# One tile in 48 fetched row by row by SyncE, beside GpSimd's gathers

## The reference

```
layer 0 (GCN):  S h, times W1, relu, S again, times W2      S: sum over edges with degree factors
layer 1:        total(h) - sum_{edges} h[src], normalized, times W
layer 2 (GCN):  edge weights edge_weight, one sum over edges
layer 3:        per edge a function of x[src], x[dst], batch norm, softmax-like weights, sum at dst
```

## Time and profile before

| | |
|---|---|
| Median of 3 runs | 11316.48 us (11309.37 to 11317.57) |
| The profiled execution | 11348.41 us, its span 11346.6 us |
| Mean granted TensorE clock | 0.597 |
| Busy: PE, PEld, DVE, ACT, POOL | 38%, 26%, 30%, 28%, 73% |
| Gathers of pass 0, 1, 2, 3, 4 begin at | 267.6, 2373.3, 4386.4, 6458.8, 8569.6 us |
| The last gather of pass 3, of pass 4 starts at | 8420.0, 10557.1 us |
| DMA, mean over the span | 94 GB/s |

### The profile page before, as it was taken

The page is one execution under the profiler, slowest core; times in us unless marked ns, Lnnn a source line. Parts: engine busy times, 40 slices in busy tenths (PEclk is TensorE's granted clock), DMA queues, the critical chain, the costliest instruction groups (busy, mean ns, idle before and its releaser), DMA issues. The chain is left out here.

```text
span 11346.6 us, 83949 instructions
## 1 busy us (share of the span) xinstructions
PE 4273.1 (38%) x19462; PEld 3000.1 (26%) x19463; DVE 3429.0 (30%) x7384; ACT 3213.0 (28%) x7261; POOL 8251.9 (73%) x8365
## 2 busy tenths in 40 slices
PE   1222222342222223223333433333354333334687
PEld 0111111121111112111111333333354333333576
DVE  4000001110001112000000422222235677777898
ACT  3333333343333334333333300000021111111465
POOL 5777777757777775777777677777766777777676
PEclk5555555665555555555555665655676555555799
DMA  4222222232222223222222212221214555555454
GB/s 104 78 79 79 79 79 79 74 87 79 79 79 79 79 79 100 78 79 79 78 78 78 62 52 52 52 52 53 53 46 137 156 159 164 164 164 168 149 168 134
DMA packets 676090, 1067.87 MB, mean 94 GB/s; under 512 B 150850, under 2 KB 518729, under 8 KB 648857
## 3 DMA queue, kind: packets, MB, share of 16 engines
q0 software_dynamic: 329072, 676.05, 22.8%
q10 hardware_dynamic: 247712, 225.10, 6.1%
q1 hardware_dynamic: 98985, 163.50, 4.4%
HBM read 904.63 MB, written 161.05 MB: 94 GB/s over the span
## 5 line engine op out<-in xcount | busy, mean ns | idle before, releaser
L447 POOL DMA_INDIRECT big<-table_parts,tile_cols x4689 | 4453.3, 950 | 1593.1 <-issue 1428.9
L604 PE MATMUL psum<-big 128*128 x4992 | 1724.3, 504 | 4129.3 <-SPq L456 4030.3
L604 PEld LDWEIGHTS psum<-big 128*128 128x128 bf16 x4992 | 663.9, 140 | 4928.4 <-issue 2683.2
L447 POOL DMA_INDIRECT big<-ptable,tile_cols x1563 | 1512.1, 967 | 498.7 <-issue 476.3
L447 POOL DMA_INDIRECT big<-table,tile_cols x1563 | 1485.9, 951 | 478.7 <-issue 476.2
L561 ACT ACTIVATE big<-big,ones 128x2048 bf16<-128x2048 bf16 x312 | 624.4, 2001 | 3707.5 <-PE psum L604 2469.5
L554 ACT ACTIVATE big<-iota_col,dl_tab 128x128 bf16<-128x128 f32 x4992 | 1490.6, 387 | 33.7 <-PEq L731 13.3
L1617 PE MATMUL psum<-acc,big 128*128 x3328 | 788.4, 420 | 1217.5 <-DVE big L1594 1205.1
L583 DVE TENSOR_REDUCE acc<-psum 128x128 f32<-128x384 f32 (+1 forms) x196 | 109.7, 560 | 3648.4 <-PE psum L608 1829.2
L677 PE MATMUL psum<-big 128*128 x3328 | 751.9, 418 | 1201.8 <-SPq L456 750.1
L1617 PEld LDWEIGHTS psum<-acc,big 128*128 128x128 f32 x3328 | 704.9, 317 | 1300.9 <-issue 1300.6
(11 more groups left out here) (300 smaller groups left out, 4274.1 us busy)
## 6 DMA issues: line engine op xcount, KB each, us to landing
big<-dl_rows ACTq DMA_DIRECT2D x104, 1024.0 KB
zrows<-big ACTq DMA_DIRECT2D x104, 1024.0 KB
big<-zrows SPq DMA_DIRECT2D x104, 1024.0 KB
big<-table_parts,tile_cols POOLq DMA_INDIRECT x4689, 2.6
table_parts<-big SPq DMA_DIRECT2D x42, 672.0 KB, 3.5
big<-table,tile_cols POOLq DMA_INDIRECT x1563, 2.5
big<-ptable,tile_cols POOLq DMA_INDIRECT x1563, 2.6
ptable<-big SPq DMA_DIRECT2D x14, 455.0 KB, 3.9
```

Source lines behind the costliest of these rows:

```text
L447: pool.indirect_dma_start(out=slots[:, t % (groups * GT), 0:width], out_offset=None, in_=tab, in_offset=bass.IndirectOffsetOnAxis(ap=idx_t ...
L604: last = nc.tensor.matmul(held, m, rows_t, start=False, stop=False, skip_group_check=True)
```

## The change

In passes 0 to 3, POOL leaves the last tile of 31 groups (8, 14, 20, ..., 188) to SP. For that tile SP issues 128 transfers, each of one row from DRAM into one partition of the ring's slot. They are spread over the six relay steps that lie between the release of the slot (group 8 + 6k uses the slots of group 6k) and the relay's landing of that group: 21 or 22 transfers in each step, behind the step's `s_free`. The byte offsets of the 128 rows are in a new table in SBUF, made once in the setup (row numbers times 768, and times 512 for pass 3), and SP loads them into registers 32 at a time. The transfers share one semaphore, `s_side`, that the relay waits for (16 x 128) and clears ahead of announcing the group. SP's part is written out, as it was; TensorE's programs stay loops. In the setup, SP issues two more loads ahead of the copies, and DVE waits for them and makes two multiplications.

```diff
+SIDE_FIRST, SIDE_EVERY = 8, 6
+SIDE_LOAD = 32
...
+    SIDE = list(range(SIDE_FIRST, TGROUPS - RGROUPS + LEAD + 1, SIDE_EVERY))
+    SIDE_SPAN = SIDE_EVERY * GT * P
+    SIDE_BASE = (SIDE_FIRST + 1) * GT * P - SIDE_SPAN
...
+        def has_side(no, g):
+            return no < PASSES - 1 and g in SIDE
...
-            return 16 * sum(tiles_of(k) for n in range(no + 1)
+            return 16 * sum(tiles_of(k) - has_side(n, k) for n in range(no + 1)
...
-                for k in range(tiles_of(g)):
+                for k in range(tiles_of(g) - has_side(no, g)):
...
-        def relay_rows(sp, no, groups, lead, s_done, done0):
+        def relay_rows(sp, no, groups, lead, s_done, done0, fetch_side=None):
             def landed(g):
                 sp.wait_ge(gathered[g % RGROUPS], landed_count(no, g))
+                if has_side(no, g):
+                    sp.wait_ge(s_side, 16 * P)
+                    sp.sem_clear(s_side)
                 sp.sem_inc(s_landed[no], 1)
...
                     sp.sem_inc(s_free, 1)
+                    if fetch_side:
+                        fetch_side(sp, g)
+
+        def side_rows(no, tab, slots, width, kind, row_bytes):
+            flat, size = tab.rearrange("n f -> (n f)").unsqueeze(0), row_bytes // width
+            numbers = []
+            def fetch(sp, g):
+                k, j = g // SIDE_EVERY, g % SIDE_EVERY
+                if k >= len(SIDE):
+                    return
+                t = SIDE[k] * GT + GT - 1
+                for e in range(j * P // SIDE_EVERY, (j + 1) * P // SIDE_EVERY):
+                    if e % SIDE_LOAD == 0:
+                        numbers.clear()
+                        words = [nc.alloc_registers(f"side{no}_{k}_{e + i}", engines=[SP]) for i in range(SIDE_LOAD)]
+                        nc.regs_load(words, side_of[kind][k:k + 1, e:e + SIDE_LOAD])
+                        numbers.extend(nc.snap(word, engines=[SP], donate=True, min_val=0, max_val=(N - 1) * row_bytes,
+                                               guaranteed_mod_val=0, out_of_modulus=row_bytes) for word in words)
+                    at = numbers[e % SIDE_LOAD] // size
+                    sp.dma_start(slots[e:e + 1, t % RSLOTS, 0:width], flat[:, bass.ds(at, width)]).then_inc(s_side, 16)
+            return fetch
...
-                    relay_rows(sp, no, RGROUPS, LEAD, s_prod, items0)
+                    relay_rows(sp, no, RGROUPS, LEAD, s_prod, items0, side_rows(no, table16, ring16, NPARTS * F, 0, 2 * NPARTS * F))
...
+                side_src = src[SIDE_BASE:SIDE_BASE + len(SIDE) * SIDE_SPAN].rearrange("(k s) -> k s", s=SIDE_SPAN)[:, SIDE_SPAN - P:]
+                for to in side_of:
+                    sp.dma_start(to, side_src).then_inc(s_last, 16)
...
-                dve.wait_ge(s_last, 32)
+                dve.wait_ge(s_last, 64)
+                nc.vector.tensor_scalar(side_of[0], side_of[0], 2 * NPARTS * F, None, ALU.mult)
+                step(nc.vector.tensor_scalar(side_of[1], side_of[1], 4 * F, None, ALU.mult))
```

More of the change, by code:

```diff
@@ L77, in gnn_kernel @@
     NTAB = NI + BODY
+    SIDE = list(range(SIDE_FIRST, TGROUPS - RGROUPS + LEAD + 1, SIDE_EVERY))
+    SIDE_SPAN = SIDE_EVERY * GT * P
+    SIDE_BASE = (SIDE_FIRST + 1) * GT * P - SIDE_SPAN
+    assert SIDE_FIRST == RGROUPS and RGROUPS - SIDE_EVERY == LEAD and SIDE_BASE + len(SIDE) * SIDE_SPAN <= E
     CHUNKS = NW // CW
@@ L180, in gnn_kernel @@
         score_tab = ew_tab[:, 0:NI]
+        side_tab = sb("side_numbers", [64 + len(SIDE), P], i32)
+        side_of = [side_tab[64 * k:64 * k + len(SIDE), :] for k in range(2)]
         rows_all = sb("rows", [13, max(7 * SCW, NI // 2, PLAN_HALVES * PLAN_WORDS)])
@@ L429, in gnn_kernel @@
         s_free = sem("rows_free")
+        s_side = sem("side_rows")
         def tiles_of(g):
             return min(GT, NT - g * GT)
+        def has_side(no, g):
+            return no < PASSES - 1 and g in SIDE
         def landed_count(no, g):
-            return 16 * sum(tiles_of(k) for n in range(no + 1)
+            return 16 * sum(tiles_of(k) - has_side(n, k) for n in range(no + 1)
                             for k in range(g % RGROUPS, g + 1 if n == no else TGROUPS, RGROUPS))
@@ L632, in _ @@
                 def _(sp):
-                    relay_rows(sp, no, RGROUPS, LEAD, s_prod, items0)
+                    relay_rows(sp, no, RGROUPS, LEAD, s_prod, items0, side_rows(no, table, ring32, F, 1, 4 * F))
                 @block.vector
@@ L914, in _ @@
                         ln.relu(act, t - 1, (t - 1) % 2)
-                act.wait_ge(s_dve, 15)
+                act.wait_ge(s_dve, 16)
                 nc.scalar.activation(deg_r, deg, ACT.Sqrt).then_inc(s_cnt, 1)
@@ L934, in _ @@
                 nc.vector.tensor_scalar(is_node[:], node_id[:, 0:NW], float(N), None, ALU.is_lt)
-                dve.wait_ge(s_last, 32)
-                step = Steps(dve, s_dve, 0, 3)
+                dve.wait_ge(s_last, 64)
+                nc.vector.tensor_scalar(side_of[0], side_of[0], 2 * NPARTS * F, None, ALU.mult)
+                step = Steps(dve, s_dve, 0, 4)
+                step(nc.vector.tensor_scalar(side_of[1], side_of[1], 4 * F, None, ALU.mult))
                 nc.vector.tensor_scalar(last_wi, last_i, P.bit_length() - 1, None, ALU.arith_shift_right)
@@ L951, in _ @@
                 dve.wait_ge(s_starts, 1)
-                step = Steps(dve, s_dve, 3, 10)
+                step = Steps(dve, s_dve, 4, 10)
                 step(nc.vector.tensor_tensor(bound[:, 0:NW], bank[5][:, 0:NW], wplus1[:, 0:NW], ALU.add))
@@ L1035, in _ @@
                         keep_dl(t - 2)
-                step = Steps(dve, s_dve, 3 + 10, 3)
+                step = Steps(dve, s_dve, 4 + 10, 3)
                 dve.wait_ge(s_degrees, 1)
@@ L1063, in _ @@
                 last.then_inc(s_counted, 1)
-                pe.wait_ge(s_dve, 3)
+                pe.wait_ge(s_dve, 4)
                 nc.tensor.matmul(bank[5][:, 0:NW], first, tile_cnt[:, 1:NW + 1], start=True, stop=True).then_inc(s_starts, 1)
```

## The result

The changed kernel takes 11159.99 us (median of 4 runs, 11154.31 to 11165.72) against 11317.02 (4 runs, 11309.37 to 11317.73) for the kernel before on the same chip: a ratio of 0.9864, 95% interval 0.9848 to 0.9879. The forecast was 11164.0. The profiled execution spans 11159.8 us.

The account below looks back on a forecast made before the run. POOL's gathers were taken as the bound. Profiled: 11348.4 - 155.6 for 124 tiles + 3 for setup = 11195.8 us; the same 152.6 off the median 11316.5 gives 11163.9, whole range 11140 to 11800.

Parts of the forecast that it names:

- What goes: POOL's gathers in passes 0 to 3: 124 tiles fewer at 1.2549 us each, 155.6 us off.
- The pace: SP's time for six groups against POOL's for 47 tiles: 59.65 us against 59.0, so SP 0.65 behind.
- T: SP's time for six groups, with 128 row transfers, register loads, relay and waits: forecast 59.65 us.
- the law: A pass loses side tiles x (T - POOL's cycle) - slack where positive; forecast as 31 x (T - 59.0) - 49 us.
- The slack: SP frees ring slots five groups ahead of POOL's need: some 49 us, covering a lag of 20 us at a pass's end.
- The address without an operation: SP's row transfers: division and multiplication of the number cancel, leaving no register operation; otherwise T = 72.9 and 12692 us.
- rival 1: SP becomes the pace because one-row transfers cost 0.297 us or more: 11743 us at 0.297, 12930 at 0.372; chance 0.22.
- Setup: Two more loads ahead of SP's copies and two VectorE steps delay the start by 3 us, bounds 0 and 5.
- From profile to median: The shown median, 11316.5 us, is 31.9 below the profiled execution; the same 152.6 us was taken off it.
- Rival 2: SP's 32-word register load costs 0.2135 us a word, so T = 78.4 and 13367 us; chance 0.05.
- Rival 3: The DMA side holds SP's issue: at 0.45 us a row, T = 71.7 and 12537 us; chance 0.06.
- Rival 4: The border: T between 60.6 and 62.2 us, so part of the gain or none; chance 0.09.

Follow-up runs that it names:

- e3: The changed kernel again, unchanged, run beside other variants: 11160.83 us, ratio 0.9864 to the kernel before.
- e7: Changed kernel with a side tile every 5 groups instead of 6, lead of 3 groups, 37 a pass: 11828.46 us, ratio 1.0439 to the kernel before.
- e4: Changed kernel with side tiles at gaps of 5 and 6 groups by turns, 34 a pass instead of 31: 11176.86 us, ratio 0.988 to the kernel before.
- e5: Changed kernel with one ALU_OP more a row, SP multiplying each number by the element's size: 11678.52 us, ratio 1.0297 to the kernel before.
- e6: Changed kernel with row numbers in the table, SP multiplying each by the row's width in a FUSED_REGOPS: 11920.24 us, ratio 1.0505 to the kernel before.
- e1: Changed kernel with SP fetching nothing: POOL leaves the 124 tiles out, their slots keep old rows: 11160.68 us, ratio 0.9865 to the kernel before.
- e2: Changed kernel with POOL gathering every tile, SP issuing its rows, 512 bytes each, into an unread tile: 11317.14 us, ratio 1.0003 to the kernel before.

## Why the prediction was right

**What goes: right.** 124 x 1.251 = 155.1 us against 155.6; measured 157.0 in the first runs, 152.6 in those of e3. The forecast of 152.6 was the same product less 3 us of setup; the ratio's interval, 0.9848 to 0.9879, is 137 to 172 us, so the total doesn't tell these apart.

**The pace: right as a sign, wrong in two terms that helped.** A transfer took 0.228 us, not 0.253; with its MOVE and gaps a row is 0.330 in the mean, not 0.356, so 128 rows are 42.3 us and not 45.6. The wait for the last row is 1.3 us and not the 2.6 of a gather's landing. The loads (four at 2.128 and gaps, 8.7) were right to 0.1, the release table's loads came at 1.03 us, not 0.9. T is thus 42.3 + 8.7 + 2.7 + 0.1 + 1.3 = 55.1 us, and not 59.65; e7, where SP runs without a pause, has 53.9 to 54.9 with one relay step fewer (an estimated 0.45 us, a sixth of the 2.7). The forecast had SP 0.65 us a cycle behind POOL and covered by the slack; in fact it is 3.7 ahead, and its cycle of 58.8 is POOL's. So the slack that the forecast leaned on was not drawn on in this kernel; it is e4 to e7 that test it. The full gain was said to end 8 ns a row above the forecast. In fact there is room for (58.8 - 55.1)/128 = 29 ns a row before SP is the slower one, and by the law for the slack's 48/31/128 = 12 ns beyond; e4, with SP 0.4 to 1.3 us a cycle behind, says that this second part is not free. e5, at +73 ns, is past it; nothing was tried between.

**The slack: right in size, not in all that was hung on it.** 49 us stated, 48 measured; that it is used up once in a pass and not once in a cycle is what the table above shows. That a lag at a pass's end costs nothing holds for lags of 14 to 30 us in e4 and fails at 42 us, where the stretch after pass 2 grew by 12.7.

**The address without an operation: right.** The forms of L506 are MOVE and transfer only. e5 and e6 show what that was worth: one operation of 33 or 37 ns a row turns 1.4% faster into 3.0% or 5.0% slower. The prediction had it as part of rival 1, with 12692 us for it at 64 ns.

**Setup: small, as said.** VectorE's step that follows the two new loads:

```profile
1.39 0.73 SPq L837 DMA_DIRECT2D big<-in_dst  x1
...
2.16 0.59 SPq L842 DMA_DIRECT2D side_numbers<-in_src  x2
...
6.25 0.17 DVE L983 TENSOR_SCALAR big<-big 128x13 int32<-128x13 int32 x1
```

This timeline (start, us) has it at 6.25 instead of 4.86, and the first gather starts at 268.8 instead of 267.6, in e3 at 267.9. But e1 and e2, with the same setup, have it at 267.6 and 267.4, so of the 3 us that were taken the start of the gathers shows nothing that stands out of its scatter of 1.4 us.

**From profile to median: right in sum.** The profiled execution of before was 32 us above its median. The gathers' length is nearly all of it: e2, whose POOL does the same, has means of 946 to 948 ns in passes 0 to 3 and not 949 to 951, and 962 in pass 4 and not 967, together 30 us over the 7815 gathers.

**The rivals.** Rival 1, a dear transfer, fell: 224 to 339 ns, median 228. Why ScalarE's took 0.297 no run shows. Rival 2, 0.2135 us a word, fell: 32 words took 2.128 us, 0.067 each, where four had taken 0.854, 0.2135 each. (Its T adds up to 78.2 us, not 78.4, which changes nothing.) Rival 3, a held issue, fell: the longest of 15,872 transfers is 339 ns, and e2's ratio is 1.0003. Rival 4, the border, isn't this kernel's, but e4 is there: without a wait at the ring, 3 tiles a pass more brought nothing.

## What to carry to other kernels

POOL's issue of gathers was the bound here, and work came off it at full price, 155 us for 124 tiles, while SP kept the pace. In a kernel like it, write down the cycle of the engine that takes work over against the bounding one's, and the slack of the ring, once for each pass. Leave room below equality: at 55.1 of 58.8 us nothing is lost, at 54.2 to 55.1 of 53.8 three tiles more a pass ended 16 us slower than without them, though the ring never ran dry, and past the slack each nanosecond of a row comes back 4 x 31 x 128 times, 16 us (e6's four windows are 226 us longer than e5's, for 14 ns a row). Look at the forms of the line for a register operation before anything else: it decided here between 1.4% faster and 3.0% slower.

## What was not expected of the hardware

- A register operation of 33 ns on SP took 70 ns of its time, gap and all; the FUSED_REGOPS of e6 took 37 ns, on the engine where L722's took 64.
- SP's row of one-row transfers was held for 0.33 us mostly once in 57 to 61 rows, 236 times in 15,872, in e5, with a register operation in each row, mostly once in 39 to 41, 348 times in all: the more instructions to a row, the fewer rows between two holds. What the sequencer does there no run shows.
- SP's loads of four words from the tables went from a median of 0.854 us to 1.032, at the same line of code and in the same number; without the rows, in e1, it is 0.855, with them, in e2, 1.032. Why the rows around them make a load longer no run shows.
- 15,872 transfers of one row of 768 or 512 bytes, one each 0.32 us, left no mark on the 7815 gathers of 128 rows beside them (946 ns with and without); the 768 bytes are the kernel after beside e1, the 512 are e2.
- The level of the gathers, 946 or 949 ns, differs between two executions whose POOL does the same (before and e2), and is worth 30 us here.
- A gather that started inside one of VectorE's MEMSETs of PSUM, with a TENSOR_TENSOR or SCALAR_TENSOR_TENSOR next on VectorE, ended 990 to 999 ns after the MEMSET's end, all 60 of them in e4, instead of 946 ns after its own start; behind a MEMSET with a COPY next none was longer than usual. Why, no run shows.
